# Edge features times weights made one layer earlier, and copied into the accumulator memory by ScalarE

## The reference

```python
ep = ef @ We + be                       # ef: edges x 64, We: 64 x 32
scores = jnp.einsum('ehd,ehd->eh', q[dst], k[src] + ep[:, None, :]) * scale
scores = scores * ew[:, None]
m = jax.ops.segment_max(scores, dst, num_segments=n)
ex = jnp.exp(scores - m[dst])
s = jax.ops.segment_sum(ex, dst, num_segments=n)
out = jax.ops.segment_sum((ex / s[dst])[:, :, None] * v[src], dst, num_segments=n)
```

## Time and profile before

| | |
|---|---|
| time, median of 3 runs | 7084.02 us (7069.73 to 7101.26) |
| the profiled execution's own time | 7118.91 us |
| its span, first to last instruction | 7117.1 us |
| mean granted TensorE clock | 0.772 |
| third layer's edges: first and last scatter start | 3173.25 and 4744.20 us |
| last layer's edges: first and last gather start | 4993.3 and 6597.2 us |
| busy over the span: PE, DVE, ACT, POOL | 64%, 59%, 40%, 58% |

### The profile page before, as it was taken

The page is one execution under the profiler, slowest core; times in us unless marked ns, Lnnn a source line. Parts: engine busy times, 40 slices in busy tenths (PEclk is TensorE's granted clock), DMA queues, the critical chain, the costliest instruction groups (busy, mean ns, idle before and its releaser), DMA issues. The chain is left out here.

```text
span 7117.1 us, 97234 instructions
## 1 busy us (share of the span) xinstructions
PE 4567.6 (64%) x17620; PEld 3413.6 (48%) x17621; DVE 4218.4 (59%) x10350; ACT 2830.5 (40%) x7829; POOL 4152.5 (58%) x3730
## 2 busy tenths in 40 slices
PE   7366666641455544775555555547578887888799
PEld 5234333320233333464444444436466666666688
DVE  4366666676555555674444444446587877887554
ACT  0133333344333333342222222223477777777543
POOL 1666666623666666238888888851566666666210
PEclk9666676775767777897777777769788888888899
DMA  6344444424555555227777777765565555565100
GB/s 200 104 106 107 108 110 107 108 85 145 178 173 173 171 176 171 77 73 105 103 105 103 104 103 105 104 134 187 163 175 168 170 172 170 170 179 171 50 32 28
DMA packets 644440, 920.30 MB, mean 129 GB/s; under 512 B 92783, under 2 KB 500943, under 8 KB 644272
## 3 DMA queue, kind: packets, MB, share of 16 engines
q0 software_dynamic: 277808, 587.53, 36.6%
q1 hardware_dynamic: 347024, 311.25, 15.0%
q10 hardware_dynamic: 19440, 19.79, 0.8%
HBM read 742.43 MB, written 175.77 MB: 129 GB/s over the span
## 5 line engine op out<-in xcount | busy, mean ns | idle before, releaser
L1667 POOL DMA_INDIRECT gcn<-c_update,c_target x832 | 1319.5, 1586 | 277.3 <-issue 217.1
L1306 PE MATMUL psum<-g_rows,g_onehot 128*128 x1664 | 622.9, 523 | 765.9 <-ACT g_rows L1221 346.8
L2043 POOL DMA_INDIRECT s_rows<-kv,s_idx x832 | 798.5, 960 | 536.5 <-PE psum L2159 252.4
L662 POOL DMA_INDIRECT e_rows<-hrow,e_idx x832 | 818.3, 983 | 484.8 <-issue 234.7
L1198 POOL DMA_INDIRECT g_rows<-x,g_idx x784 | 765.4, 976 | 423.8 <-issue 229.6
L1306 PEld LDWEIGHTS psum<-g_rows,g_onehot 128*128 128x128 f32 x1664 | 387.1, 254 | 1001.7 <-issue 948.4
L725 PE MATMUL psum<-e_rows,e_onehot 128*128 128x265 f32 x1664 | 653.1, 546 | 298.7 <-DVE acc L819 116.2
L1615 PE MATMUL psum<-c_same,c_onehot 128*128 128x128 f32 x1664 | 361.5, 385 | 650.9 <-DVEq L1593 650.9
L1615 PEld LDWEIGHTS psum<-c_same,c_onehot 128*128 128x128 f32 x1664 | 307.2, 276 | 752.7 <-DVEq L1593 415.0
L725 PEld LDWEIGHTS psum<-e_rows,e_onehot 128*128 128x128 f32 x1664 | 385.8, 258 | 508.4 <-issue 213.5
L1274 DVE TENSOR_TENSOR acc<-acc,psum 128x256 f32 x832 | 349.5, 420 | 419.3 <-issue 199.7
(11 more groups left out here) (358 smaller groups left out, 9245.0 us busy)
## 6 DMA issues: line engine op xcount, KB each, us to landing
g_attr<-in_edge_attr SPq DMA_DIRECT2D x196, 512.0 KB
c_srow<-rows_src SPq DMA_DIRECT2D x208, 256.0 KB
e_drow<-rows_dloc SPq DMA_DIRECT2D x208, 128.0 KB
s_drow<-rows_dloc SPq DMA_DIRECT2D x208, 128.0 KB
s_feat<-in_edge_feat SPq DMA_DIRECT2D x832, 32.0 KB
n_sums<-gcn SPq DMA_DIRECT2D x100, 256.0 KB
e_rows<-hrow,e_idx POOLq DMA_INDIRECT x832
gcn<-c_update,c_target POOLq DMA_INDIRECT x832
```

The lines of the kernel that those rows point to most:

```text
L662: pool.indirect_dma_start(rows[u][:, s, 0:D + H], None, k.hrow, bass.IndirectOffsetOnAxis(ap=idx[u][:, s:s + 1], axis=0)).then_inc(gathere ...
L1306: pe.matmul(k.psum[:, s, 0:D], onehot[q % 2][:, s, :], rows[:, bass.ds(m[q % 2 * GROUP + s], 1), :].rearrange("p o d -> p (o d)"), start=T ...
L1667: pool.indirect_dma_start(k.gcn[a], bass.IndirectOffsetOnAxis(ap=target[q][:, a:a + 1], axis=0), update[q][:, a, :], None, compute_op=ALU. ...
L2043: pool.indirect_dma_start(rows[at.u][:, st, 0:2 * D], None, k.kv, bass.IndirectOffsetOnAxis(ap=idx[at.u][:, st:st + 1], axis=0)).then_inc( ...
```

## The change

The product of edge features and weights moves out of `att_edges` into `gcn_edges`. There SP loads the features of each group (four DMAs), PE makes the four products right after `mix_group`'s, ACT copies them to SBUF (128x128) after `c_mix`, and SP stores them to HBM (64 KB) three groups later. In `att_edges` SP loads the products of a group with one DMA in place of four, and ACT copies them into the bank that PE wrote before, between `weigh` of group g-6 and `mark`, one group ahead of `add_features`. PE has no part in it any more.

```diff
 def gcn_edges
+        ROWS_BANK, BEHIND = 6, 3
+            def load_feat(g, q):
+                wait_if_any(sp, rows_done, g - RING + 1)
+                i = load_indices(nc, sp, k.step_i, g * GROUP, GROUP, EA_TILES - 1)
+                for s in range(GROUP):
+                    sp.dma_start(feat[q][0:EDGE_D, s, :], edge_feat[:, bass.ds(i[s] * P, P)]
+                                 ).then_inc(feat_landed[q], 16)
+            def store_rows(g, q):
+                sp.wait_ge(rows_copied, g + 1 + 2)
+                sp.dma_start(k.edge_rows[bass.ds(g, 1)].rearrange("o p n -> p (o n)"), edge_rows[q][:]
+                             ).then_inc(rows_stored[q], 16)
...
                                  ).then_inc(srow_landed[q], 16)
+                    load_feat(g, q)
+                    if not isinstance(it, int) or q >= BEHIND:
+                        store_rows(g - BEHIND, (q - BEHIND) % RING)
...
                 ins.then_inc(mixed, 1)
+                pe.wait_ge(feat_landed[q], (it + 1) * (16 * GROUP))
+                pe.wait_ge(rows_copied, g + 1)
+                for s in range(GROUP):
+                    ins = pe.matmul(k.psum[:, ROWS_BANK + b, s * HEAD_D:(s + 1) * HEAD_D], feat[q][:, s, :], we_sb[:],
+                                    start=True, stop=True)
+                ins.then_inc(rows_done, 1)
...
                 act.copy(mix[b][:], k.psum[:, b, :]).then_inc(mix_ready, 1)
+                act.wait_ge(rows_done, g + 1)
+                wait_if_any(act, rows_stored[q], it * 16)
+                act.copy(edge_rows[q][:], k.psum[:, ROWS_BANK + b, 0:GROUP * HEAD_D]).then_inc(rows_copied, 1)
 def att_edges
-            def load_feat(at):
-                wait_if_any(sp, ep_done, at.g - GB + 1)
-                i = load_indices(nc, sp, k.step_i, at.g * GROUP, GROUP, EA_TILES - 1)
-                for s in range(GROUP):
-                    sp.dma_start(feat[at.q][0:EK - 1, s, :], edge_attr[:, bass.ds(i[s] * P, P)]
-                                 ).then_inc(feat_landed[at.q], 16)
+            def load_rows(at):
+                wait_if_any(sp, rows_moved, at.g - GB + 1)
+                sp.dma_start(edge_rows[at.q][:], k.edge_rows[bass.ds(at.g, 1)].rearrange("o p n -> p (o n)")
+                             ).then_inc(rows_landed[at.q], 16)
...
+            def move_rows(at):
+                act.wait_ge(rows_landed[at.q], (at.n + 1) * 16)
+                wait_if_any(act, ep_added, at.g)
+                act.copy(k.psum[:, EP, 0:GROUP * DH], edge_rows[at.q][:]).then_inc(rows_moved, 1)
...
                         weigh(at)
+                    if Group(n, q, 1).live:
+                        move_rows(Group(n, q, 1))
+                    if at.live:
                         mark(at)
...
             def look_up(at):
-                pe.wait_ge(feat_landed[at.q], (at.n + 1) * (16 * GROUP))
-                wait_if_any(pe, ep_added, at.g)
-                for s in range(GROUP):
-                    ins = pe.matmul(k.psum[:, EP, s * DH:(s + 1) * DH], feat[at.q][:, s, :], we_sb[:],
-                                    start=True, stop=True)
-                ins.then_inc(ep_done, 1)
...
             def add_features(at):
-                dve.wait_ge(ep_done, at.g + 1)
+                dve.wait_ge(rows_moved, at.g + 1)
```

More of the change, by code:

```diff
@@ L1564, in _ @@
                                  ).then_inc(srow_landed[q], 16)
+                    load_feat(g, q)
+                    if not isinstance(it, int) or q >= BEHIND:
+                        store_rows(g - BEHIND, (q - BEHIND) % RING)
+            for g in range(PASSES * RING - BEHIND, PASSES * RING):
+                store_rows(g, g % RING)
+            for q in range(RING):
+                sp.wait_ge(rows_stored[q], 16 * PASSES)
         @block.vector
@@ L1655, in _ @@
         def _(pool):
+            for q in range(RING):
+                ins = pool.memset(feat[q][EDGE_D:EDGE_D + 1, :, :], 1.0)
+            ins.then_inc(ones_ready, 1)
             pool.sem_inc(passed, (RING - 1) * GROUP)
@@ L1917, in att_edges @@
         drow = [sb(f"s3_drow{q}", [P, GROUP * P], BF16) for q in range(GB)]
-        feat = [sb(f"s3_feat{q}", [EK, GROUP, P]) for q in range(GB)]
+        edge_rows = [sb(f"s3_edge_rows{q}", [P, GROUP * DH]) for q in range(GB)]
         spread = [sb(f"s3_spread{b}", [P, GROUP * P]) for b in range(2)]
@@ L2025, in _ @@
                         load_dst(ahead)
-                        load_feat(ahead)
+                        load_rows(ahead)
                     if q == 2 and Group(n, q).live:
@@ L2031, in _ @@
         def _(pool):
-            for q in range(GB):
-                ins = pool.memset(feat[q][EK - 1:EK, :, :], 1.0)
-            ins.then_inc(ones_ready, 1)
             def gather(at):
```

36 lines of the change are left out of this document (22 added, 14 removed).

## The result

The changed kernel takes 6910.95 us (median of 4 runs, 6899.85 to 6913.82) beside 7078.19 us for the kernel before on the same chip (4 runs, 7069.73 to 7101.26): ratio 0.9754, 95% interval 0.9738 to 0.9769, or 167 us less. The forecast was 72 us less. A second measurement on another chip gave 0.9771 (0.9755 to 0.9787). The direction held, and the time is 6 us above the lower end of the range (6905 us); the size was off by a factor of 2.3.

What follows compares the result with a forecast made beforehand. POOL's scatter issuing was taken to bound the third layer, and a ring of waits, followed on DVE, the last. 76 us gained there less 4 lost in the third gave -72 us from 7084.02: 7010 us, range 6905 to 7110.

Steps and rivals of the forecast that it cites:

- PE is held by L2139 at q=0 and q=1 of DVE's steps, and not at the others: Last layer's edges: the removed product L2139 delays the queries twice a block, and is hidden at q=2 and q=3.
- The walk: Last layer: one block's timeline followed with L2139 gone; 2.3 us gained, 0.8 taken back by ACT, 1.5 us a block left.
- With the 4.2 us that they now take: Last layer, queries of q=2: start at 5869.6, keep 4.2 us, are through at 5873.8 instead of 5876.14.
- q=0 unchanged: Last layer, q=0: ACT's copy comes 0.9 us late, but DVE's 1.6 us wait for the scan hides it.
- ACT's chain takes back 0.8 us at q=3: Last layer: add_features of q=3 waits for ACT's copy behind weigh, starting at 5879.2 rather than 5878.4.
- The clock kept: Last layer: PE's granted clock, 0.86, stays although 4.9 us of matmuls leave each block, since the long idle before L2168 remains.
- The third layer costs 4 us: Third layer: PE, ACT and DMA additions are hidden; SP's loads before the first c_srow cost 0 to 10 us, taken as 4.
- 1: Last layer: ACT's copy costs and PE gives nothing back; add_features of q=3 0.8 us late, +46 us, 7130 us; chance 0.1.
- 2: Last layer: the clock falls, one more half-clock stretch a block at q=3, 150 us, 7162 us; chance 0.06.
- 3: Third layer pays: late scatters or SP at 8 us a group, the stage growing by 92 us, 7104 us; chance 0.06.
- rival 4: Last layer: DVE's waits before L2306 and L2231, 4.4 us a block, all go: 227 us, 6860 us (half, 6970); chance 0.1.
- three signs of being wrong: Copy's wait over 1.5 us a block, stage's granted clock under 0.8, or scatters over 1.65 us.

Runs made afterwards that it cites:

- x14: Kernel before, last layer, edge products left out at q=3 and q=0 from the second block on: ratio 0.9998, on the chip where the kernel before takes 6558 us.
- x18: Kernel before, last layer, edge products left out at q=1 and q=2 from the second block on: ratio 0.9895, where the kernel before takes 7076 us.
- x13: Kernel before, last layer, edge products left out at q=1 and q=2 from the second block on: ratio 0.9926, where the kernel before takes 6558 us.
- x4: Changed kernel without ACT's copy in the last layer, DVE adding the loaded products straight from SBUF: ratio 0.9826 to the kernel before.
- x5: x4 with four unread products of the old shape put back on PE ahead of the queries, waiting for nothing: ratio 0.984 to the kernel before.
- x1: Kernel before with only the last layer's half of the change, loading stand-in rows for the stored products: ratio 0.9791.
- x2: Kernel before with only the third layer's half of the change, the last layer still making the products on PE: ratio 0.9969.
- x8: Kernel before, third layer, SP issuing the c_srow load only after ACT has copied the update of the group in turn: ratio 0.9976.
- x15: Kernel before, last layer, no edge products from the second block on and no ACT copy: ratio 0.9927, where the kernel before takes 6558 us.
- x17: Changed kernel as it is, measured again on another chip, where the kernel before takes 7076 us: ratio 0.9771.
- x16: Changed kernel with four unread PE products ahead of the queries of q=1 and q=2, behind look_up's waits: ratio 1.0143, where the kernel before takes 6558 us.
- x6: x4 with eight unread 128x128 PE products behind turn, in the wait for the scan: ratio 0.9676 to the kernel before.
- x9: Kernel before with eight unread 128x128 PE products at q=0 of the last layer's edges, ahead of the wait for the scan: ratio 0.9983.
- x10: Changed kernel with eight unread 128x128 PE products at q=0, ahead of the scan's wait, ACT's copy there waiting for them: ratio 0.9752 to the kernel before.

## Why the prediction was right and wrong

- *PE is held by L2139 at q=0 and q=1 of DVE's steps, and not at the others:* right. Dropping the other two changed nothing (x14, on the fast chip). Alone this is worth 1.5 us a block on chips like the first (75 us in x18), 1.0 on the fast one (50 us in x13). The walk had 2.3 before ACT's part.
- *"With the 4.2 us that they now take":* this is the step that failed. The 4.2 us from L2145's start to its reader weren't the queries' own time to be kept, but 2.0 us and some 2.1 us of lateness that comes with the products (x4 against x5) and left with them. The queries of q=2 are through after 2.03 us. The walk's 5873.8 should have been about 5871.6, so that DVE no longer waits at q=2 and is bound by its own work there: 5.57 us, against a smallest step of 5.37. With that the prediction's own rows give more: ACT would be done at 5871.6 + 5.10 + 0.3 = 5877.0 and holds nobody, DVE starts its sums at 5873.82, and the next `add_features` comes at 5873.82 + 4.33 = 5878.15 in place of 5880.72. That is 2.6 us a block, 134 us, where 1.5 us and 76 were forecast and x1 measured 148. The prediction saw both numbers, 1.97 and 4.2, and took the larger as fixed without asking what made it. Why the queries come late with the products stays open (see the last section).
- *q=0 unchanged:* wrong. The step went from 10.45 to 9.29 us, and the scan's wait from 1.57 to 0.85 (x2 against x1: 9.91 to 9.33, and 1.15 to 0.69). Argued, not tried: less delay is handed round the ring from block to block, while the walk followed one block from a fixed start.
- *ACT's chain takes back 0.8 us at q=3:* right in kind. q=3 is the one step that got longer, 6.18 to 6.48 us, and the wait there for the sums 0.28 to 0.46; the end of `weigh` stands 0.63 us ahead of `add_features` in the median at q=3 and 0.68 at q=0, which is the copy and its semaphores. The copy took 254 ns (taken: 0.3).
- *The clock kept:* it didn't fall, 0.90 for 0.86. The row shows it rising while PE's busy time fell from 244 to 220 of 300 us (196 were forecast, for blocks of the old length), and in the third layer it fell from 0.73 to 0.70 while PE's busy time rose from 172 to 226. The Trainium skill, as the prediction used it (TensorE: Matmul & The Clock Gate, Part 1: The HAM clock gate), would let the clock follow the activity; by the mean of a stretch, neither stage here shows that.
- *The third layer costs 4 us:* wrong in sign, 22 us gained (x2). This is the second term that was mis-sized, 26 of the 95 us missing. "POOL's own issuing is the stage" was right; what was missed is that a scatter's 1586 ns aren't all its own: the commonest scatter takes 1550, and 23 ns of the mean went when fewer started in DVE's one-hot. The loads at the stage's start, taken at 4 us, cost at most 2: the first scatter starts at 3144.0 us in x2 and at 3142.1 in x1. The Trainium skill (DMA: Bandwidth & Descriptors, Issuing engines are not separate DMA queues) says that transfers of all issuers share the engines, and the prediction used it for a loss only. x8 agrees that a plain load's moment sets a scatter's landing (4.7 us against 4.0 with the load sent later), and so there was a gain to be had.
- *Rivals:* 1, 2 and 3 did not occur. 6911 us lies in rival 4's part of the range, below the forecast's own 6960, and that had a chance of 0.1: of 4.4 us of waits before L2306 and L2231 1.9 are left.
- *Signs:* DVE's idle before L2306 (0.9 us a block, "about 1"), PE's wait in the third layer (1.3 us less, "1 to 2") and the scan's wait came as forecast. Four scatters took 7.47 us and not 7.56, and the steps sum to 27.5 us and not 29.3. None of the three signs of being wrong appeared: they watched for losses alone.

What stays open: x18 leaves 89 us to the changed kernel on the same chip, of which the third layer gives some 22; the rest is 1.3 us a block. Between them lie the products of q=3 and q=0, the copy and the order of ACT's stream. x14 and x15 say that those two products are free on the fast chip; on a chip like the first they weren't taken out, and the late results (14 of 43 in x18, 0 of 42 in x17) suggest that they aren't there. That was argued, not tried. The changed kernel without anything added wasn't run on the fast chip, so what the change gives there isn't known: x16 bounds it only from above.

## What to carry to other kernels

Where an instruction's row says 2 us and its reader starts 4 us after it, find out what the second half is before you keep it or drop it in a sum; put the work back alone in front of it and look at the reader. When an experiment shows no effect, compare the means of the other instructions too: here 2 us of returned waits were hidden by an addition that became 0.6 us faster, and the same addition made a filler for the clock look useful. When one trace is of an execution above the median, check a stretch that the change doesn't touch before you read differences off it. And in a stage bound by one engine's fixed issue, a mean that is 1 or 2% above the commonest duration is a gain that can be had: look at which other engine's work starts with the long ones.

## What the hardware showed that was not expected

- *Chips differ by 8 to 9% on this program, and not everywhere.* 6558 us against 7076 to 7133. First to last indexed DMA of the four edge stages: first layer 1071 us against 1302 (before), second 1025 against 1178, third 1572 against 1571, last 1446 (x14, which measured as before) against 1604.
- *Recorded and real speed of PE.* On the slower chips the q=2 queries with a recorded 1.97 us were read some 4.2 us after their start in 26 of 28 cases in before, while of 19 whose record is over 3.2 us, as at half clock, one was over 1 us late. In all 26 the recorded clock had risen from 1.2 to 2.4 GHz between 3.9 and 4.9 us before the queries started; for the two that weren't late it had risen 22 us before. 3.4 us is what the row L2145 has at half clock, and L2139 loses 0.84 more. So these products may well have run at half clock with a record of full clock; that is an inference. On the fast chip a recorded 1.97 was read after 2.01, though the recorded clock had risen 4.6 us before in the median (x14). The Trainium skill (TensorE: Matmul & The Clock Gate, Seeing it yourself) warns that the clock's trace events have been unreliable on trn2; this fits it but doesn't prove it here, and it limits what the half-clock sums of x6, x9 and x10 can say.
- *Semaphore records are missing on the slower chips.* In the profile of before 46% of PE's and 28% of DVE's increments have no record within 0.25 us of the instruction's end, nearly all of them ahead of 3000 us or in the last edge stage; in x14 99% are there. Waits named "remote" or after an old transfer in these stages go back to that, and a reader's start is the better evidence.
- *An addition with both sources in SBUF takes twice as long when it meets a multiplication of POOL's:* 2734 ns against 1227 (x4), while from the accumulator memory it takes 1221 beside the same instruction (after). POOL's gathers take 1026 ns in the mean in x4 and 960 in the changed kernel. The Trainium skill (SBUF — State Buffer, SBUF: two separate sides) names the pair: an operation of DVE with two SBUF inputs and one of POOL that reads SBUF exclude each other on a shared port pair. The trace agrees: the addition's end stands 1.09 us behind the multiplication's in every one of the long ones. The page gives the pair to the operation that starts first; by the records it is the addition that starts first, by 0.4 us in the median, and the addition that waits.
